# Piecewise-linear GELU computed without the clamp of its input and without the identity step

## The reference, cut to what matters

```python
_PWL_X = jnp.linspace(-4.0, 4.0, 33)
_PWL_Y = 0.5 * _PWL_X * (1.0 + erf(_PWL_X / sqrt(2.0)))

def pwlin_gelu_basic(x, mantissa_bits_in, mantissa_bits_out):
    xq = float2fix(x, mantissa_bits_in)          # round to multiples of 2**-8
    y = jnp.interp(xq, _PWL_X, _PWL_Y)
    y = jnp.where(xq > 4.0, xq, jnp.where(xq < -4.0, 0.0, y))
    return float2fix(y, mantissa_bits_out)

h = float2fix(x @ w1 + b1, 8)                    # 1024 tokens x 512
h = float2fix(pwlin_gelu_basic(h, 8, 8), 8)
out = float2fix(h @ w2 + b2, 8)
```

## Time and profile before

| | |
|---|---|
| time, median of 3 runs | 469.24 us (469.21 to 469.24) |
| the profiled execution's own time | 466.66 us |
| span of the profiled execution | 464.5 us |
| PE busy | 386.0 us (83%) |
| DVE busy | 333.9 us (72%) |
| ACT busy | 242.6 us (52%) |
| POOL busy | 195.8 us (42%) |
| mean granted TensorE clock | 0.931 |

### The profile page before, as it was taken

How to read it: one execution, slowest core, us unless ns; L and a number is a source line. 1 busy time by engine, 2 the same in 40 slices (tenths; PEclk the granted TensorE clock), 3 DMA queues, 4 the chain that set the end, 5 groups by cost and what they waited for, 6 DMA issues and landing times.

```text
span 464.5 us, 8292 instructions
## 1 busy us (share of the span) xinstructions
PE 386.0 (83%) x2778; PEld 222.9 (48%) x2778; DVE 333.9 (72%) x676; ACT 242.6 (52%) x474; POOL 195.8 (42%) x252
## 2 busy tenths in 40 slices
PE   7758799998589848996898789998999779999940
PEld 3415445564366435552544344543445546676630
DVE  5765594657865799879898999888841686667642
ACT  3614356556624641475376557664676454565520
POOL 5125987544645492744327206460440004113114
PEclk9856999999989999997999599998999979999995
DMA  7572708026107106422044103520030001402112
GB/s 178 132 184 54 159 15 189 1 55 150 35 1 207 34 0 142 108 70 68 1 128 111 47 1 111 128 69 23 25 109 1 6 13 59 126 28 67 43 42 62
DMA packets 44766, 34.67 MB, mean 75 GB/s; under 512 B 5965, under 2 KB 41229, under 8 KB 44429
## 3 DMA queue, kind: packets, MB, share of 16 engines
q1 hardware_dynamic: 43701, 32.03, 26.9%
q0 software_dynamic: 1024, 2.10, 1.5%
HBM read 15.11 MB, written 7.86 MB: 49 GB/s over the span
## 4 chain that ended last, share of the span: by engine, by line
PE 43%; DVE 22%; issue 11%; DMA 9%; ACT 5%; SPq 4%; POOL 4%; POOLq 0%; DVEq 0%; ACTq 0%
PE p_sc L606 6%; DVE mx L879 6%; PE p_misc L576 5%; PE p_o L625 4%; DMA slots_in<-qx,kx 4%; PE p_misc L507 3%; SPq L1434 3%; PE p_o L638 3%; PE p_misc L781 3%; PE p_sc L781 3%; PE p_misc L533 2%; PE p_misc L680 2%; DVE xn L849 2%; PE p_o L792 2%; POOL slots_in L1360 2%
## 5 line engine op out<-in xcount | busy, mean ns | idle before, releaser
L879 DVE TENSOR_REDUCE mx<-p_misc 128x1 f32<-128x512 f32 x192 | 122.4, 684 | 26.0 <-PE p_misc L576 24.4
L1190 ACT ACTIVATE probs<-p_sc 128x512 f32<-128x512 f32 x192 | 104.4, 597 | 59.8 <-PE p_sc L606 59.2
L576 PE MATMUL p_misc<-kS,qS 96*128 96x512 f16 x128 | 41.8, 400 | 10.8 <-DVE mx L879 10.8
L1304 POOL TENSOR_SCALAR veps<-meanvar 128x2 f32<-128x2 f32 x16 | 3.9, 246 | 103.2 <-DVE meanvar L835 102.8
L606 PE MATMUL p_sc<-qS,kS 128*128 128x256 f16 x256 | 42.4, 284 | 2.3 <-ACT probs L1190 1.6
L1346 POOL TENSOR_TENSOR psums<-probs 128x256 f32<-128x256 f32 x32 | 25.3, 792 | 42.3 <-PE p_o L632 38.5
L638 PE MATMUL p_o<-probs,v 128*32 128x256 f32 x512 | 41.9, 406 | 0.5 <-issue 0.3
L1101 DVE TENSOR_TENSOR probs<-probs,p_sc 128x512 f32<-128x512 f32 x30 | 20.6, 687 | 24.8 <-ACT probs L1268 23.0
L625 PE MATMUL p_o<-probs,v 128*64 128x256 f32 x256 | 34.7, 391 | 4.3 <-ACT probs L1190 4.3
L1372 POOL DMA_INDIRECT probs<-slots_out,kx x16 | 15.1, 946 | 48.6 <-DMA slots_out<-probs 38.6
L1268 ACT ACTIVATE probs<-p_misc 128x512 f32<-128x512 f32 x30 | 17.9, 597 | 32.8 <-PE p_sc L781 31.8
(11 more groups left out here) (210 smaller groups left out, 770.4 us busy)
## 6 DMA issues: line engine op xcount, KB each, us to landing
region<-kx SPq DMA_DIRECT2D x24, 256.0 KB, 3.9
v<-in_L_ffn_W_dram SPq DMA_DIRECT2D x24, 256.0 KB, 2.7
region<-qx SPq DMA_DIRECT2D x24, 128.0 KB, 3.9
slots_in<-qS SPq DMA_DIRECT2D x2, 960.0 KB, 7.0
slots_out<-probs SPq DMA_DIRECT2D x30, 64.0 KB
kS<-kS SPq DMA_DIRECT2D x1, 1664.0 KB
kS<-k_scratch SPq DMA_DIRECT2D x8, 192.0 KB
kS<-slots_in SPq DMA_DIRECT2D x6, 256.0 KB, 3.4
```

The costliest lines, as they stand in the source:

```text
L576: pe.matmul(ps, q[:, i * P:(i + 1) * P], k, start=True, stop=True).then_inc(full, 1)
L879: dve.tensor_reduce(mx[:, b % 2, i, h:h + 1], ps, AX_X, ALU.max).then_inc(free, 1)
L1190: act.activation(probs[:, h % 8, half * 512:(half + 1) * 512], p_sc[:, half, :], ACT.Exp, scale=(DH0 if layer == 0 else DH1) ** -0.5).then ...
```

## The change

The clamp (line 928) goes, and `floor` reads N where it read the clamped Y1. `identity` becomes one instruction: line 951 rounds G straight into N and releases PE; line 952 goes. Values outside [-4, 4] are then interpolated between Gelu nodes beyond that interval. All steps keep their places in `order`, and no wait is added. Each of the four batches has two DVE instructions on 128 x 1024 f32 fewer.

```diff
                 link(dve.tensor_scalar(N, N, MAGIC, MAGIC, ALU.add, ALU.subtract))
-                link(dve.tensor_scalar(Y1, N, -4 * FIX, 4 * FIX - 1, ALU.max, ALU.min))
 
             def floor(b):
 
                 N, F, G, Y1 = (fixed[b // 2][:, i, :] for i in range(4))
-                link(dve.tensor_scalar(G, Y1, -(STEP - 1) / 2, BREAK, ALU.add, ALU.add))
-                dve.scalar_tensor_tensor(F, G, BREAK, Y1, ALU.subtract, ALU.subtract).then_inc(breaks, 1)
+                link(dve.tensor_scalar(G, N, -(STEP - 1) / 2, BREAK, ALU.add, ALU.add))
+                dve.scalar_tensor_tensor(F, G, BREAK, N, ALU.subtract, ALU.subtract).then_inc(breaks, 1)
                 dve.wait_ge(breaks, b + 1)
...
             def identity(b):
 
                 N, F, G, Y1 = (fixed[b // 2][:, i, :] for i in range(4))
-
-                link(dve.tensor_scalar(G, G, MAGIC, MAGIC + 4 * FIX - 1, ALU.add, ALU.subtract))
-                dve.scalar_tensor_tensor(N, N, 4 * FIX - 1, G, ALU.max, ALU.add).then_inc(hidden, 1)
+                dve.tensor_scalar(N, G, MAGIC, MAGIC, ALU.add, ALU.subtract).then_inc(hidden, 1)
                 dve.wait_ge(hidden, b + 1)
```

## The result

The changed kernel takes 455.47 us (median of 5 runs, 454.5 to 458.45) beside 469.21 us of the kernel before: a ratio of 0.9723, 95% interval 0.9686 to 0.976. The prediction was 459.4 us with a range of 456.6 to 463.0 us. In three later groups of runs the kernel before had medians of 468.96, 468.94 and 467.9 us, and in the last of them the changed kernel had 455.79 us, so the saving is 12 to 14 us.

The account below looks back on a forecast made before the run. DVE was taken to set the pace in the GELU stretches, PE elsewhere. The terms 1.66 + 1.5 + 1.66 + 1.57 + 1.24 + 1.02 + 1.13 = 9.8 us gave 469.24 - 9.8 = 459.4 us, range 456.6 to 463.0 us.

Parts of the forecast that it names:

- batch 0: line 952 and the clock: Down projection: PE's 3.02 us gap shrinks by 1.66 us; clock stays up, saving 1.5 us (bounds 0 and 1.5).
- batch 1: clamp and line 952: Clamp gives nothing, at most 0.72 us; line 952 gives 1.66 us of PE's 3.05 us wait.
- batch 2: clamp and line 952: Clamp gives 1.57 us, at least 0.72; line 952 gives 1.24 us of PE's wait before its down projection.
- batch 3: clamp and line 952: Clamp gives 1.02 us, at least 0.72; line 952 gives 1.13 us, PE's whole wait for the maximum behind it.
- The working for POOL's neighbourhood in batch 2: Without the clamp, line 933 inherits its 1.53 us beside POOL; line 934 ends about 210.75 us instead of 212.32.
- third case: Where POOL stretched DVE's instructions, only their undisturbed price returns: 6.3 us saved, 462.9 us, or 461.4 with the clock; chance 0.16.
- fifth and sixth cases: Fifth: slower, PE's clock falls and stays down from 272 to 300 us. Sixth: no change, a transfer sets the path. Each 0.03.
- Batch 1, clamp: nothing: Line 934 ends as ACT's Gelu table load ends, so ACT starts no earlier without the clamp: 0, at most 0.72 us.
- at most 0.5 us: Batch 3's clock: PE's gap stays above 3 us, so the return of slow products was counted as nothing.
- the median of the runs is 2.6 us above the profiled execution: Whole kernel: the same difference taken for both kernels, so 469.24 - 9.8 = 459.4 us.
- fourth case: More than the sum: stretches at 1.2 GHz behind PE's gaps shrink too, up to 12.9 us saved, 456.3 us; chance 0.13.
- the distance from batch 3's maxima to the end: From 272 us to the span's end, 192 us: a change of over 1 us would make the prediction wrong.

Follow-up runs that it names:

- idle matmuls: Matmuls on data already there, result unread, put into five of PE's gaps: kernel before 467.5 us beside 468.94 us without them, changed kernel 457.45 us.
- six buffers: Six instead of four buffers for the experts' results: kernel before 467.76 us beside 468.96 us with four, changed kernel 454.89 us (ratio 0.9694).

## Why the prediction was wrong in size

PE's lead, by batch, against the steps of the prediction:

| step | forecast, us | first profile, us | second profile, us |
|---|---|---|---|
| batch 0: line 952 and the clock | 1.66 + 1.5 | 3.2 | 3.2 |
| batch 1: clamp and line 952 | 0 + 1.66 | 2.1 | 2.1 |
| batch 2: clamp and line 952 | 1.57 + 1.24 | 2.8 | 3.1 |
| batch 3: clamp and line 952 | 1.02 + 1.13 | 2.8 | 2.7 |
| lead at 390 us, start included | 9.8 | 11.3 | 11.9 |
| given back behind 390 us | 0 | 3.1 | 1.6 |

**What held.** Batch 0 came out to the tenth: 1.66 us, then the clock stayed up and line 680 took 2.02 us. The working for POOL's neighbourhood in batch 2 held as well: line 932 inherited 1.53 us, line 933 ended where the sum put it, and the clamp gave 1.50 us. In the changed kernel's second profile the meeting was another one:

```profile
201.50 0.98 DVE L932 TENSOR_SCALAR region<-region 128x1024 f32<-128x1024 f32 x1
202.52 2.06 DVE L933 SCALAR_TENSOR_TENSOR region<-region 128x1024 f32<-128x1024 f32 x1
```

That is the sign named for the third case, line 933 at over 2 us, and batch 3 has it too. But the lead grew by 1.8 us at this place, not by 0.72, so the sign came without the case. In all seven profiles without batch 2's clamp the lead grows by 1.5 us or more at this place, and in the six others by -0.2 to 0.8 us. So the third case falls. The rule behind it (the Trainium skill, page "SBUF — State Buffer", section "SBUF: two separate sides") is not contradicted: POOL's instructions still hold up DVE's (1.53 us for line 932, 0.69 us undisturbed). What comes back depends on which of them meet, 1.5 us in the first profile and 1.8 us in the second, and 0.8 us of it can come with no instruction removed. PE is still full between 262 and 290 us, and the fifth and sixth cases did not occur.

**The clamp of batch 1.** The step "Batch 1, clamp: nothing" looked at the wrong engine. As it said, ACT gained nothing: the Gelu starts 2.85 us earlier than before, which is PE's lead behind batch 0. But DVE did not wait for the Gelu. In the kernel before it goes from line 934 to six maxima and reaches line 940 only at 165.09 us, when ACT had been done with the nodes since 163.8:

```profile
161.50 3.68 DVE L879 TENSOR_REDUCE mx<-p_misc 128x1 f32<-128x512 f32 x6
...
165.09 1.64 DVE L940 TENSOR_TENSOR kS<-kS 128x1024 f32<-128x1024 f32 x1
```

DVE has no idle time from 158 us to line 952, and line 680 waits for line 952. So an instruction taken out anywhere in this stretch comes through whole; that PE's earlier wait, for ACT, grew from 2.53 to 3.26 us has no weight. This is 0.8 us; 0.35 us of batch 1's gain was lost again on DVE's work right behind it, so the batch gave 0.4 us more than forecast. In the second profile PE no longer waited there at all, and the batch gave the same 2.1 us.

**Batch 3.** Line 952 gave 1.6 us, not 1.13. The prediction took PE's idle time as the limit. But from the start of the product of line 576 ahead of that wait to the start of the one behind it there were 1.75 us in the kernel before, and 0.22 us in the changed one: beside the 1.13 us of waiting, the first product took 0.62 us at a clock of 0.50, and without a wait the next one starts before its end. This is the "at most 0.5 us" that was counted at nothing. The clamp gave 1.2 us, not 1.02.

**The step that failed** is the last one: "the median of the runs is 2.6 us above the profiled execution; I take the same difference for both kernels". On the scale of profiled executions the forecast for the changed kernel was 456.9 us, and its two took 458.45 and 456.36 us. That these lie on both sides of the forecast is partly luck: PE's lead was 1.5 and 2.1 us larger than the sum, and 3.1 and 1.6 us were given back. On the scale of medians the kernel before stands 2.6 us above its profiled execution and the changed one 0.6 to 3.0 us below its own. So the 2.6 us belong to the kernel before. What the profiles show for them is products at 1.2 GHz in batch 3, at times in batch 1 and at 180 us, 1.4 to 1.7 us each time, which the first profile was spared. In the profiles without line 952 those of batches 1 and 3 do not occur, and the gaps ahead of them are shorter (at most 0.3 us in batch 3). That such products fill the whole distance to the median is an inference from few profiles, and the attempt to take them away with idle matmuls did not bring the median down by that much. That was the fourth case. It had a chance of 0.13 and its far end was 456.3 us, where the median is 455.5 to 455.8. Two things spoke for it: the profiled execution lay below all runs shown, so it lacked something that they had, and the rows already showed one gap of 3.05 us that passed and one of 3.02 us that did not the earlier trace rows. Gaps that may go either way have a price in the median even where the profile shows none.

On this the Trainium skill, page "TensorE: Matmul & The Clock Gate", section "Part 1: The HAM clock gate", says that the number of slow products at a kernel's start is run-variable for one and the same kernel, since the monitor runs free of it. The starts here agree (PE's clock from 25 to 42 us was 0.51 and 0.70 in two executions of the kernel before), and the rows 3.05 us, then 2.05 or 3.78 us, show the like in the middle of a kernel.

**What the sum is now.** About 11 us of lead by removed instructions and batch 0's clock, up to 0.7 us more where before waited for a fetch near 345 us, about 2 us of stretches at 1.2 GHz that the median execution of before has and its first profile has not (an estimate: 1.6 us in 6 of 8 profiles for batch 3, 1.7 us in 2 of 8 for batch 1, 1.4 us in 2 of 8 at 180 us), less 1.6 us given back at the end: about 12 us. Measured are 12.1 us in the last group and 13.7 in the first. What fills the last microsecond or so of the first group stays open; the start alone moves an execution by up to 1.8 us, the runs of before scatter over 6 to 7 us in each later group, and six buffers (0.9 us less than the changed kernel's 455.79, in another group) suggest that the loss at the end is not the same in every execution. The mean granted clock of an execution is of little help here: over 170 executions its correlation with the time, within a kernel, is -0.32, which may be because not every stretch at 1.2 GHz costs something: those near 168 and 221 us lie under PE's waits, and from 452 us in the kernel before PE computes nothing.

**The end of the experts** was in no step: a lead on PE brings its last expert's work up against the fetch and the stores of SyncE, which wait for transfers that did not get faster. PE came there 11.3 and 11.9 us earlier, the fetch of line 1505 only 9.3 and 10.6 us. With four buffers PE's wait there was 2.69 and 2.16 us in the two profiles; with six it was 0.76 us. The long indirect transfer is only a part of this: POOL waited 3.98 us for it in the first profile and 3.36 us in the second, but in the kernel with the short identity step and idle matmuls PE's wait was 2.15 us with POOL's at 1.61 us. The prediction had named a sign for this step: the distance from batch 3's maxima to the end, 192 us, should not change by over 1 us. It grew by 2.4 and 1.5 us. The changed kernel with six buffers, 454.89 us, is the fastest kernel of the study, though not by more than the scatter.

## What to carry to other kernels

Where the profiled execution is faster than the median, look for what the median has more of before you carry the difference over: PE's gaps behind which the clock sometimes falls, here gaps of 1.5 to 3.05 us, can have a price in the median, and a change that shortens them can earn it. Take a second profile of the kernel before, and look at the start of it too. For an instruction removed from a busy queue, ask first which engine is never idle from there to the product that the path waits for; waits of other engines in between don't matter. And follow a lead to the end of the kernel, where queues of transfers give part of it back.

## What the chip showed that was not expected

One gap of PE of 3.05 us was followed by products at 2.4 GHz in one execution and at 1.2 GHz in two others of the same work (2.05, 3.78 and 3.79 us). Matmuls put into a gap so that only 1.49 us of it were idle did not keep the clock up in one execution (3.60 us) and did in another kernel's (2.02 us). And one DVE instruction fewer gave back 1.5 us at one place in one execution and 1.8 us in another, and in a third kernel 0.8 us came back there with none removed, as other instructions of DVE and POOL ran side by side.
